# Graph attention and mean aggregation on one core: masks made for two code tiles at a time, and ScalarE taking part of VectorE's work at the end

## The reference

```
h  = relu(layernorm(x)); h0 = h
for i in 0, 1:                                  # two attention layers
    Wh = h @ W[i]; u = Wh @ L1 @ a; v = Wh @ L2 @ a
    e  = leaky_relu(u + v.T + lb @ a, 0.2)
    h  = 0.2 * h0 + 0.8 * elu(softmax(where(adj > 0, e, -9e15), axis=1) @ Wh)
x  = x + concat(h0, h1, h2) @ mlp_w + mlp_b
h  = relu(layernorm(x))
x  = x + concat((adj == 1) @ h / deg, h) @ weight + bias
```

## Time and profile before

| | |
|---|---|
| median of 3 runs | 1733.85 us (1733.81 to 1733.99) |
| the profiled execution | 1734.81 us, its span 1733.0 us |
| layer 0, first to last mask matmul | 83.4 to 849.0 us |
| layer 1 | 869.6 to 1469 us |
| last phase | 1469.5 to 1733 us |
| PE busy | 1538.9 us (89%) |
| DVE busy | 1531.3 us (88%) |
| ACT busy | 1289.1 us (74%) |

### The profile page before, as it was taken

The page is one execution under the profiler, slowest core; times in us unless marked ns, Lnnn a source line. Parts: engine busy times, 40 slices in busy tenths (PEclk is TensorE's granted clock), DMA queues, the critical chain, the costliest instruction groups (busy, mean ns, idle before and its releaser), DMA issues. The chain is left out here.

```text
span 1733.0 us, 50280 instructions
## 1 busy us (share of the span) xinstructions
PE 1538.9 (89%) x21783; PEld 1495.0 (86%) x21783; DVE 1531.3 (88%) x2480; ACT 1289.1 (74%) x1470; POOL 82.2 (5%) x118
## 2 busy tenths in 40 slices
PE   2477888888888888888799999999999999799999
PEld 2377888788888888787699999999999999799999
DVE  7899999999999999999798787869688788986665
ACT  3777898989899998989699999999999994000000
POOL 1100000101010000101100000000000000000000
PEclk9589999999999999999899999999999999999999
DMA  7988999999999999997211212122121111133231
GB/s 272 356 310 311 385 378 401 356 410 376 411 372 407 387 375 407 363 410 275 61 45 44 56 45 63 42 59 62 39 63 50 57 51 32 57 116 89 86 94 44
DMA packets 114701, 356.02 MB, mean 205 GB/s; under 512 B 8976, under 2 KB 17200, under 8 KB 114480
## 3 DMA queue, kind: packets, MB, share of 16 engines
q1 hardware_dynamic: 91040, 304.27, 46.2%
q0 software_dynamic: 8960, 29.43, 6.2%
q10 hardware_dynamic: 14480, 19.11, 3.1%
HBM read 325.45 MB, written 27.33 MB: 204 GB/s over the span
## 5 line engine op out<-in xcount | busy, mean ns | idle before, releaser
L498 ACT ACTIVATE region<-ub,bigv 128x1024 uint8<-128x1024 f32 x1024 | 1096.0, 1149 | 28.6 <-PE bank L1644 11.3
L1638 PE MATMUL bank<-wsplit,region 128*128 128x195 bf16 x8192 | 788.5, 250 | 41.3 <-DVE region L919 35.4
L1638 PEld LDWEIGHTS bank<-wsplit,region 128*128 128x128 fp8e3 x8192 | 695.2, 99 | 52.8 <-DVE region L919 35.3
L1644 PE MATMUL bank<-wsplit,region 128*128 128x130 f16 x8192 | 557.7, 221 | 52.2 <-DVE region L929 50.8
L1644 PEld LDWEIGHTS bank<-wsplit,region 128*128 128x128 fp8e3 x8192 | 500.5, 98 | 77.3 <-DVE region L929 72.5
L929 DVE SCALAR_TENSOR_TENSOR region<-region 128x512 uint32<-128x512 uint32 x512 | 343.5, 691 | 9.4 <-PE bank L1644 8.6
L919 DVE SCALAR_TENSOR_TENSOR region<-region 128x512 uint32<-128x512 uint32 x512 | 338.0, 691 | 10.1 <-ACT region L498 9.9
L941 DVE TENSOR_SCALAR region<-region 128x4096 uint8<-128x4096 int32 x128 | 294.1, 2297 | 0.9 <-DMA region<-in_adj 0.9
L1865 PE MATMUL bank<-wsplit,region 128*128 128x129 f16 x4032 | 239.6, 222 | 8.8 <-DVE region L1447 8.8
L1865 PEld LDWEIGHTS bank<-wsplit,region 128*128 128x128 fp8e3 x4032 | 237.5, 99 | 10.0 <-DVE region L1447 10.0
L1447 DVE TENSOR_SCALAR region<-region 128x512 uint32<-128x512 uint32 x256 | 100.4, 424 | 43.6 <-PE bank L1865 38.4
(11 more groups left out here) (223 smaller groups left out, 686.2 us busy)
## 6 DMA issues: line engine op xcount, KB each, us to landing
region<-in_adj SPq DMA_DIRECT2D x128, 2048.0 KB, 11.3
region<-codes_d SPq DMA_DIRECT2D x128, 256.0 KB, 2.6
codes_d<-region ACTq DMA_DIRECT2D x64, 256.0 KB, 6.5
ub<-u_d POOLq DMA_DIRECT2D x16, 512.0 KB, 7.5
hg<-h_d POOLq DMA_DIRECT2D x16, 256.0 KB, 6.3
stg<-m_d POOLq DMA_DIRECT2D x16, 256.0 KB, 4.8
region<-in_x SPq DMA_DIRECT2D x4, 512.0 KB, 6.9
h_d<-wsplit POOLq DMA_DIRECT2D x4, 512.0 KB, 4.2
```

Of the source, the lines that this page charges most:

```text
L498: last = nc.scalar.activation(sv[:, b, :], ub[G % 2][:, :], ACT.Relu, bias=bigv[l][:, t:t + 1], scale=BIG)
L1638: return nc.tensor.matmul(acc_on[it], columns(onb[U % NS], it, b), wsplit[:, c * TC + 2 * q + b, 0:WC], start=(c == 0 and q == 0 and b == ...
L1644: return nc.tensor.matmul(acc_off[it], columns(offb[U % NO], it, b), woff[:, c * TC + 2 * q + b, WO:WO + WF], start=(c == 0 and q == 0 and ...
```

## The change

- **Masks of two tiles.** A unit is now one bit position of a pair of tiles (n even, n + 1). `onb` has four and `offb` three buffers of 4 KB in place of eight and six of 2 KB, the code buffers are read in pairs (`ptp`), and `on_mask` and `off_mask` are one instruction on 1024 uint32. A unit has four ramps instructions (two for each tile, `h` = 0, 1) and 32 + 32 matmuls. Even steps handle bit positions 0 and 1 of the pair, odd steps 2 and 3. All buffer waits count units of the new kind.
- **One more tile ahead in layer 0.** A pair's first unit needs the codes of both tiles, so DVE converts and packs tile n + 4 in step n (tile 3 and the first pair's masks of bit positions 0 and 1 come ahead of the loop), PE transposes tile n + 3, ACT takes tile n + 2. `take_codes(n)` waits for `pair_done(n - NP)`: all masks of the pair that the old tile belongs to.
- **Splits.** `split_first` handles the first two subtiles of both tiles 0 and 1, `split` the other six of each, both ahead of the loop; in step n, chunk n + 2 is split, and ACT casts chunk n + 1 in its step n.
- **The last groups.** At the end ACT does, of groups 5 to 7: the copies of transposed h (`take_last_h3`, `take_last_h2`), the evacuation of y (`take_y`), the casts (`cast_y`, `high_last_h3`, `high_last_h2`), and the clip before the last exponential. The order of DVE's and PE's pieces there is written anew.

```diff
-LU = QC * NT
+LU = 2 * NT
...
-NA, NP, NS, NO = 3, 4, 8, 6
+NA, NP, NS, NO, NM = 3, 4, 4, 3, 8
...
+        ptp = [at(58 * KB + 4 * i * KB, 4 * KB, U8) for i in range(NP // 2)]
+        onb = [at(66 * KB + 4 * i * KB, 4 * KB, U8) for i in range(NS)]
+        offb = [at(82 * KB + 4 * i * KB, 4 * KB, U8) for i in range(NO)]
...
+        def pair_done(M):
+
+            return 2 * (M - M % 2 + 2)
...
                 def take_codes(n):
                     act.wait_ge(tp_done, n + 1)
                     if n >= NP:
-                        act.wait_ge(off_r, 4 * (n - NP) + 4)
+                        act.wait_ge(off_r, pair_done(n - NP))
                         act.wait_ge(c_st[n % NP], 16 * (n // NP))
...
# ACT, layer 0
                 for n in range(NT):
                     g, r = n // NCH, n % NCH
-                    ramps(0, n, 0)
-                    if g == 0 and r > 0:
-                        cast_high(0, r)
-                    ramps(0, n, 1)
-                    if n + 1 < NT:
-                        take_codes(n + 1)
+                    ramps(0, n, 0, 0)
+                    if 0 < n < NCH - 1:
+                        cast_high(0, n + 1)
+                    ramps(0, n, 0, 1)
+                    if 0 < n < NT - 2:
+                        take_codes(n + 2)
                     if r == 5 and g > 0:
                         high(NG + g - 1)
-                    ramps(0, n, 2)
...
+                    ramps(0, n, 1, 0)
+                    if 0 < n < NT - 2:
+                        store_codes(n + 2)
+                    if 0 < n < NCH - 1:
+                        cast_middle(0, n + 1)
+                    ramps(0, n, 1, 1)
...
# ACT, layer 1
+                    ramps(1, n, 0, 0)
+                    if n < NCH - 1:
+                        cast_high(1, n + 1)
+                    ramps(1, n, 0, 1)
+                    ramps(1, n, 1, 0)
+                    if n < NCH - 1:
+                        cast_middle(1, n + 1)
+                    ramps(1, n, 1, 1)
...
+                take_last_h3(5)
+                cast_y(4)
+                take_y(5, 0, tpb)
+                take_y(5, 1, tpb)
+                cast_y(5)
                 row_exp(2 * NG - 1)
+                high_last_h3(6)
+                take_last_h3(6)
+                high_last_h2(7)
+                take_y(6, 0, tpb)
+                take_y(6, 1, bank[6])
+                cast_y(6)
+                take_last_h2(7)
+                high_last_h3(7)
+                take_last_h3(7)
+                take_y(7, 0, tpb)
+                take_y(7, 1, bank[6])
+                cast_y(7)
...
# DVE, ahead of layer 0's loop
                 split_first(0)
+                dve.wait_ge(p_in, 2)
+                on_mask(0, 0, 0)
+                off_mask(0, 0, 0)
                 split(0, 0)
+                split(0, 1)
                 row_args(0)
                 convert(2, 1)
                 pack_pairs(2)
                 pack(2)
+                on_mask(0, 0, 1)
+                off_mask(0, 0, 1)
+                convert(3, 0)
+                convert(3, 1)
+                pack_pairs(3)
+                pack(3)
                 for n in range(NT):
                     g, r = n // NCH, n % NCH
-                    ahead = n + 3 < NT
-                    dve.wait_ge(p_in, n + 1)
-                    if n + 1 < NCH:
-                        split_scaled(0, n + 1)
-                    on_mask(0, n, 0)
-                    on_mask(0, n, 1)
-                    off_mask(0, n, 0)
-                    if n + 1 < NCH:
-                        split_rest(0, n + 1)
+                    ahead = n + 4 < NT
+                    if n > 0 and n % 2 == 0:
+                        dve.wait_ge(p_in, n + 2)
+                    if n + 2 < NCH:
+                        split_scaled(0, n + 2)
+                    if n > 0:
+                        on_mask(0, n, 0)
+                    if n + 2 < NCH:
+                        split_rest(0, n + 2)
                     if ahead:
-                        convert(n + 3, 0)
-                    off_mask(0, n, 1)
+                        convert(n + 4, 0)
+                    if n > 0:
+                        off_mask(0, n, 0)
...
                     if ahead:
-                        convert(n + 3, 1)
+                        convert(n + 4, 1)
...
+                    if n > 0:
+                        on_mask(0, n, 1)
...
-                        pack_pairs(n + 3)
+                        pack_pairs(n + 4)
...
+                    if n > 0:
+                        off_mask(0, n, 1)
                     if ahead:
-                        pack(n + 3)
-                    if n + 1 < NCH:
-                        split_last(0, n + 1)
+                        pack(n + 4)
+                    if n + 2 < NCH:
+                        split_last(0, n + 2)
...
# DVE, layer 1
                 split_first(1)
                 split(1, 0)
+                split(1, 1)
...
                 for n in range(NT):
+                    if n + 2 < NCH:
+                        split_scaled(1, n + 2)
                     if n > 0:
                         on_mask(1, n, 0)
-                        on_mask(1, n, 1)
                         off_mask(1, n, 0)
-                        off_mask(1, n, 1)
+                    if n + 2 < NCH:
+                        split_rest(1, n + 2)
...
                     if n > 0:
-                        on_mask(1, n, 2)
-                        on_mask(1, n, 3)
+                        on_mask(1, n, 1)
...
-                        off_mask(1, n, 2)
-                        off_mask(1, n, 3)
+                        off_mask(1, n, 1)
+                    if n + 2 < NCH:
+                        split_last(1, n + 2)
...
# PE
                     for it in range(IT):
...
-                        for b in range(2):
-                            last = on_matmul(l, n, q, it, b)
+                        for h in range(2):
+                            for b in range(2):
+                                last = on_matmul(l, n, s, h, it, b)
...
-                        pe.wait_ge(p_in, min(n + 3, NT))
+                        pe.wait_ge(p_in, min(n + 4, NT))
```

More of the change, by code:

```diff
@@ L266, in nth, with tile @@
         def nth(l, c):
-            return c if l == 0 else NCH - 2 + c
+            return 6 * l + c - 1
+        def pair_done(M):
+            return 2 * (M - M % 2 + 2)
+        def tile(buf, h):
+            return buf[:, 2 * KB * h:2 * KB * (h + 1)]
         def columns(buf, it, b):
@@ L615, in _ @@
                     g, r = n // NCH, n % NCH
-                    for q in range(QC):
-                        ramps(1, n, q)
-                        if g == 0 and r > 1 and q == 0:
-                            cast_high(1, r)
-                        if g == 0 and r > 1 and q == 2:
-                            cast_middle(1, r)
+                    ramps(1, n, 0, 0)
[6 more added lines that the diff above has]
+                    ramps(1, n, 1, 1)
                     if n == 3:
@@ L849, in split_first, with ends, four @@
                 def split_first(l):
-                    on, off = expv[:, 0:2, 0:1].to_broadcast([P, 2, CE]), expv[:, 0:2, 1:2].to_broadcast([P, 2, CE])
-                    part = [wsplit[:, 0:2, j * CE:(j + 1) * CE] for j in range(3)]
-                    hi, lo = woff[:, 0:2, WO:WO + CE], woff[:, 0:2, WO + CE:WO + WF]
-                    full, rest, small = av[:, 0:2, :], bb[:, 0:2, :], po[:, 0:2, :]
+                    def ends(ap):
+                        return ap.rearrange("p (c k) e -> p c k e", c=2)[:, :, 0:2, :]
+                    def four(buf):
+                        return buf[:, 0:4, :].rearrange("p (c k) e -> p c k e", c=2)
+                    both = slice(0, 2 * TC)
+                    on, off = [ends(expv[:, both, i:i + 1]).to_broadcast([P, 2, 2, CE]) for i in range(2)]
+                    part = [ends(wsplit[:, both, j * CE:(j + 1) * CE]) for j in range(3)]
+                    hi, lo = ends(woff[:, both, WO:WO + CE]), ends(woff[:, both, WO + CE:WO + WF])
+                    full, rest, small = four(av), four(bb), four(po)
                     dve.wait_ge(scl, l + 1)
@@ L863, in split_first @@
                     ec.sync()
-                    sc.mark(nc.vector.tensor_tensor(full, hw[:, 0:2, :], on, ALU.mult))
-                    sc.mark(nc.vector.tensor_tensor(small, hw[:, 0:2, :], off, ALU.mult))
+                    sc.mark(nc.vector.tensor_tensor(full, ends(hw[:, both, :]), on, ALU.mult))
+                    sc.mark(nc.vector.tensor_tensor(small, ends(hw[:, both, :]), off, ALU.mult))
                     sc.sync()
@@ L1885, in _ @@
                 multiply_h3(5, 1, tpb)
-                for s in range(1, 6):
+                for s in range(1, 7):
                     mean_half(s)
@@ L1895, in _ @@
                 mean_half(8)
+                claim_b7()
+                transpose_h2(7, tpb)
                 mean_half(9)
                 claim_b7()
[L1898 to L1900 removed]
```

(1 more changed line is left out.)

330 lines of the change are left out of this document (179 added, 151 removed).

## The result

The changed kernel takes 1782.58 us (median of 4 runs, 1780.52 to 1783.08) against 1733.83 for the kernel before (4 runs): a ratio of 1.0281, 95% interval 1.0268 to 1.0294, 49 us slower. Forecast were 1770, range 1746 to 1790, slower at 0.88. The profiled execution took 1780.52 us, the shortest of the four; its span is 1778.6 us, 45.6 more than before. The table divides these 45.6 us; all times in it are in us.

What follows compares the result with a forecast made beforehand. DVE was taken to bound layer 0 and the 58 us after layer 1, PE the rest. Terms -17 + 24 + 16 + 4 + 2 + 13 - 6 = +36 on 1734.8 gave 1771, stated as 1770, range 1746 to 1790.

Steps and rivals of the forecast that it cites:

- Merged masks, 0.07 us each: DVE in layer 0: each merge saves 0.07 us, a step falls from 10.95 to 10.67 us; -17 us over 60 steps.
- The second rival: A mask costs its whole duration, so 240 merges at 0.152 us give -36, not -17; 1751 us, chance 0.04.
- The code buffer at r = 0, +24: Layer 0's seven group changes: ACT's wait for codes delays ramps, DVE stalls at r = 1; 2.9 + 6 x 3.5 us.
- The waits of PE costed at nothing: Layer 0, from r = 5: PE waits for take_codes(n + 3) before using bank 7 for h; costed at nothing.
- Splits of the first group, +16: Layer 0's first group: DVE's splits wait for ACT's casts behind the code wait; 9.6 + 4.0 + 1.4 + 0.9 us.
- +6 for the tile ahead and the first splits: Layer 0: one more tile converted and packed ahead, +4 us, and the two first splits, +2 us.
- the DMA share of 1.03: Layer 0: transfers are near their limit too, though hardly any instruction waits for them; no term in the sum.
- From layer 0 to layer 1, +13: Late ACT delays sums_out +3 us, first splits leave 1, third unit loses 6 idle and 2 at low clock.
- 6 us of idle PE: Start of layer 1: third unit's mask comes 10.6 us after the last split, where PE has 4.5 us of work.
- The last four steps of layer 0: Nothing holds DVE, ACT is late; PE ends its last unit at about 38.9, sums_out starts at 39.4 us.
- The end, -6: Last phase: eighteen DVE instructions, 7.5 us, go to idle ACT; PE gets back 6 us (-10 to -1).
- Mostly beside a `pick`: Last phase: each moved instruction passes a semaphore to ACT and back, mostly while a pick runs.

Runs made afterwards that it cites:

- late_turns: Changed kernel, but in step r = 0 of layer 0's seven later groups ACT issues take_codes after the step's last ramps; 1785.98 us.
- late_all: Changed kernel, but in every even step of layer 0 ACT issues take_codes after the step's last ramps; 1755.50 us.
- rows_first: late_all, but in steps r = 5, 6, 7 and 0 PE does h's transposes and products before transposing tile n + 3 of the codes; 1756.45 us.
- light_late: late_all with a quarter of each adj load left out from the fourth load on, for timing alone; 1747.94 us.
- light_before: Kernel before the change with a quarter of each adj load left out from the fourth load on, for timing alone; 1732.58 us.
- all_moves: Changed kernel with the moves of late_all, rows_first, layer1_start and tail_picks together; 1755.04 us.
- layer1_start: Changed kernel, but ACT makes the third unit's ramps before weight_exps and cast_high(1, 2), and DVE masks that unit before splitting chunks 2 and 3; 1780.75 us.
- all moves and lighter loads: all_moves with a quarter of each adj load left out from the fourth load on, for timing alone; 1745.88 us.
- tail_picks: Kernel before with only the last groups' change, plus pick_half(8) ahead of x_and_y(6, .) and pick_half(10) ahead of new_x(7); 1730.91 us.

## Why the forecast was right, and where it missed

- **Direction and main cause: right.** The pairs' code buffers hold ACT back. Taking the codes later in the even steps gives back 27.1 of the 49 us, 11.4 at the splits of the first group and some 16 after it.
- **Merged masks, 0.07 us each: right.** A step with nothing else in it is 10.68 us (forecast 10.67, before 10.96). The terms that the forecast wrote out add up to 10.93 and 10.65, not 10.95 and 10.67; their difference, 0.28, is right. The second rival took a mask to cost its whole duration. The Trainium skill's (N + 151)/0.96 (page "VectorE: DVE Perf Modes", section on the TRN2 errata) is such a duration, given there for an fp32 `tensor_tensor`; taken as the distance between masks it makes the step an estimated 10.33 us (10.96 less 4 x 0.157), and the trace's 10.68 does not agree. The prediction also left out that the page's section "The DRAIN you can't avoid" itself says that a next operation that is not held starts earlier, and with this the trace agrees: 1.13 us from start to start for a duration of 1.22. Layer 1 gained 1.4 us at most from the merges; nothing was forecast.
- **The code buffer at r = 0, +24: size right, working partly wrong.** The step r = 0 took 13.50 us at the first change of group and 14.12 or 14.13 at the six others, against 14.2: 2.8 + 6 x 3.44 = 23.5 us over 10.68, where 2.9 + 6 x 3.5 = 23.9 were forecast. But the sum was made as if the one wait at r = 0 did it. late_turns contradicts this, and late_all shows that it is the waits of all even steps. That they keep ACT from gaining the lead with which it used to absorb the copies is how the timelines read.
- **The waits of PE costed at nothing.** "I cost that at nothing, since PE has 9.1 + 0.5 us of work in a step of 10.67" is wrong in its rows: PE waits 29.0 + 22.6 us for `take_codes` in front of h's pieces (7.2 in the kernel before). It is nearly right in the time: taking this wait away moved it to DVE's `pack` (rows_first). That both orders give the same is measured; that bank 7 is the reason is argued from who waits for whom.
- **Splits of the first group, +16, and +6 for the tile ahead and the first splits: right in the sum.** Step 8 came at 214.2, forecast 214.5. The part of the code wait in it is 11.4; the forecast had 13.6 (9.6 + 4.0) for it. So what remains, the tile ahead and the other splits, took some 2 us more than forecast, and the agreement of the sum is partly luck.
- **Missed: the loads.** Steps 8 to 60 took 6.5 us more than forecast. DVE waits there 7.5 us for loads of `adj`, against 0.9 in the kernel before, and 6.4 of them stand outside the stalls at r = 0, nearly all at r = 4 and 5 (12.07 and 11.06 us, against 11.35 and 10.68 in light_late). The first paragraph of the forecast read the DMA share of 1.03 and then put no price on it. In the kernel before, the loads are just in time (at most some 1.5 us in light_before). That shorter steps, and gaps that shift the convert, make them late is argued: the changed kernel itself was not run with lighter loads, only late_all and all_moves were.
- **From layer 0 to layer 1, +13: measured +11.1** (turn 22.6 against 20.6, the rest in the first units). The "6 us of idle PE" before the third unit is there (5.74), but its cause, the mask behind the splits, isn't its price: layer1_start took that wait away and gained 1.8. That the whole of what the first units need, splits, casts and masks, sets the unit of tiles 2 and 3 fits its trace, but no run takes this work away. The step that failed here is to price a wait by its own length.
- **The last four steps of layer 0:** 40.7 us, not 38.9. ACT's lateness came as forecast: DVE's first sum of `sums_out` starts 39.6 us after step 60's first mask (forecast 39.4). But PE begins the last eight units 2.3 us after that mask and needs 38.6 us for them, with only 0.90 us idle in front of a mask, so its own work sets the 40.7.
- **The end, -6: measured -1.5, mis-sized.** DVE did lose 4 us of work in the 58 us. "Mostly beside a `pick`" was the wrong step: DVE stands 1.65 and 1.49 us for products that now need ACT in between. Putting picks into these waits gave 1.3 us back, and moving the first y gave nothing. PE's waits that are left are for the picks; what would make those faster was not tried.
- **What stays open.** With all moves and lighter loads 11.8 us remain against the kernel before, and 13.3 against light_before. In the traces of these two light kernels step 8 comes 10.8 us late, steps 8 to 60 are only 2.7 us shorter, since DVE stands 11.1 us there, 11.0 of it for PE's transposes, and all that follows is 7.5 us longer. The 10.8 us are put down to the tile converted ahead and the first splits of two chunks, which no experiment undid. late_all and all_moves vary by some 3 to 5 us from run to run, so differences under 2 us between those kernels are not read.

The fastest kernel that computes the reference's result is the one before with the tail of tail_picks: 1730.91 us, 0.18% under the kernel before (interval 0.09% to 0.27%), a size at the edge of what can be told here.

## What to carry to other kernels

A merged instruction saves only its fixed part, here 0.07 us of 1.2, and it coarsens every buffer that it reads: ask of each of them what now has to wait for the later half. An engine can win its lead in many steps and spend it in one, so a single wait relaxed where the stall shows may give nothing, while here all of them together gave half of the loss. Compare waits over the same stretch of the kernel: a shorter window made one look as if it had gone. Where a second resource stands at a share of 1.0 without a wait, give a faster step no credit below its pace until it is tested with less traffic.

## What the runs showed of the hardware

- The off mask that reads the on mask right before it starts 1.33 us after it (877.93 to 879.26 in the trace after); an operation that does not depend on the one before starts 1.13 us after one of the same size (598.39 to 599.52). The dependence, with the semaphore that carries it, costs 0.2 us more.
- With a quarter less of each load of `adj`, the DMA share goes from 1.00 to 0.84 at 309 GB/s instead of 390 (late_all, light_late). The kernel before, at 0.80 to 0.82 then, gains at most some 1.5 us in all, and its convert takes 2.30 us with both loads: at a share of 1.0 DVE's instructions were not slowed.
- At the start of layer 1 a group of 32 matmuls took 4.71 us behind a stretch in which PE was mostly idle (the last 4.87 us wholly), 2.87 us behind 1.24 us of idle time, and 4.15 us behind 5.74 us. The granted clock, a mean of its two levels of 1.2 and 2.4 GHz, is 0.65 of the higher one in the 30 us from 880, where PE is busy for 11.71 us, and 0.90 in the next 30, where it is busy for 22.56.
